# Reordering the second scan, down weights split once, and low parts of act on GpSimd, in a Mamba-2 layer kernel

## The reference, cut to what matters

```python
h = rmsnorm(x, ln1_w)
zxbcdt = h @ w_in.T                    # z, xs, B, C, dt
xBC = silu(causal_conv4(xBC) + conv_b)
dt = softplus(dt + dt_bias); a = -exp(A_log) * dt
# scan over 4 chunks of 128 rows, 4 heads, state carried from chunk to chunk:
#   Yd = ((C B^T) * decay) @ (x dt);  state = g * state + B^T (decay_end x dt);  Yo = (C state) * exp(cs)
h = x + (((Yd + Yo + D x) * silu(z)) @ w_out.T)
h2 = rmsnorm(h, ln2_w)
h = h + (silu(h2 @ gate_w.T) * (h2 @ up_w.T)) @ down_w.T        # inner width 1792 = 14 tiles
x = layernorm(x + h)
# second FFN with ternary weights, q(w) = round(clip(w / (mean|w| + eps), -1, 1)) * mean|w|, inner width 1376 = 11 tiles
x = layernorm(x + ((x @ q(w_gate).T) * (x @ q(w_up).T)) @ q(w_down).T)
```

## Time and profile before

| | us |
|---|---|
| median of 3 runs | 534.54 (533.47 to 535.83) |
| the profiled execution's own time | 534.14 |
| its span, first to last instruction | 532.3 |
| TensorE busy | 482.1 |
| DVE, POOL, ACT busy | 334.3, 252.0, 237.0 |
| mean granted TensorE clock | 0.978 |

### The profile page before, as it was taken

One profiled execution on the slowest core, in us unless ns is written; L12 is line 12 of the kernel. 1 busy time (PEld: TensorE's weight loads), 2 busy tenths in 40 slices (PEclk: granted clock), 3 DMA queues, 4 the chain that ended last, 5 costly groups with the idle time before them and its releaser, 6 DMA issues.

```text
span 532.3 us, 6133 instructions
## 1 busy us (share of the span) xinstructions
PE 482.1 (91%) x2060; PEld 378.7 (71%) x2060; DVE 334.3 (63%) x502; ACT 237.0 (45%) x438; POOL 252.0 (47%) x256
## 2 busy tenths in 40 slices
PE   6989999989779589899999989999898998999995
PEld 4767677756547467688877767887686786888884
DVE  4695777545564456658898879989944754332133
ACT  5577777565454536663333143435822331022300
POOL 5554575463732525766877554546403233123221
PEclk9999999989998969999999999999999999999998
DMA  7522021021211223443233214441410200110002
GB/s 249 186 82 79 6 75 60 20 78 61 81 64 54 79 100 135 151 171 118 81 118 120 79 66 172 158 166 72 138 61 1 78 21 0 41 39 1 1 1 79
DMA packets 15439, 44.47 MB, mean 84 GB/s; under 512 B 2480, under 2 KB 2480, under 8 KB 15408
## 3 DMA queue, kind: packets, MB, share of 16 engines
q1 hardware_dynamic: 15408, 44.08, 23.7%
HBM read 41.97 MB, written 2.10 MB: 83 GB/s over the span
## 4 chain that ended last, share of the span: by engine, by line
PE 66%; DVE 16%; issue 7%; ACT 4%; POOL 4%; DMA 2%; SPq 0%; POOLq 0%; DVEq 0%; ACTq 0%
PE psA L1553 8%; PE psA L1554 8%; PE psA L1347 5%; PE psA L1349 4%; PE psB L1562 4%; PE psB L1563 4%; DVE act_hl L1233 3%; PE psA L1335 3%; PE psA L1340 3%; PE psA L1336 3%; PE psA L1353 2%; PE psA L1355 2%; DVE q L1269 2%; PE psB L1528 1%; PE psB L1335 1%
## 5 line engine op out<-in xcount | busy, mean ns | idle before, releaser
L1553 PE MATMUL psA<-xT_h,q_gu 128*128 128x512 f32 x176 | 70.2, 399 | 1.5 <-DVE x L1281 1.5
L1554 PE MATMUL psA<-xT_l,q_gu 128*128 128x512 f32 x176 | 69.1, 392 | 0.0
L681 POOL TENSOR_TENSOR beta<-wsum,beta 128x512 fp32r<-128x512 f32 x28 | 38.9, 1411 | 37.3 <-ACT beta L844 37.3
L774 POOL TENSOR_TENSOR int_l<-prod_t,int_h 128x512 fp32r<-128x512 f32 x22 | 28.9, 1313 | 52.0 <-ACT int_h L987 51.9
L715 POOL TENSOR_TENSOR wst<-raw,wst 128x1024 fp32r<-128x1024 f32 x14 | 35.7, 2550 | 35.8 <-ACT wst L797 35.8
L982 ACT ACTIVATE gate_t<-psA 128x512 f32<-128x512 f32 x22 | 13.2, 598 | 83.0 <-PE psA L1554 83.0
L1299 DVE TENSOR_TENSOR prod_t<-gate_t,psA 128x512 f32<-128x512 f32 x22 | 15.1, 688 | 47.3 <-PE psA L1554 43.0
L1553 PEld LDWEIGHTS psA<-xT_h,q_gu 128*128 128x128 f32 x176 | 33.1, 188 | 10.2 <-issue 2.0
L1554 PEld LDWEIGHTS psA<-xT_l,q_gu 128*128 128x128 f32 x176 | 33.1, 188 | 7.3
L1233 DVE TENSOR_TENSOR act_hl<-act,act_hl 128x512 fp32r<-128x512 f32 x28 | 35.1, 1282 | 4.3 <-ACT act_hl L967 4.2
L1562 PE MATMUL psB<-q_dn,int_h 128*128 128x512 f32 x88 | 34.3, 390 | 2.1 <-issue 2.1
(11 more groups left out here) (234 smaller groups left out, 1386.0 us busy)
## 6 DMA issues: line engine op xcount, KB each, us to landing
raw<-in_f_gu_t SPq DMA_DIRECT2D x22, 512.0 KB, 3.2
raw<-in_w_gu_t SPq DMA_DIRECT2D x14, 512.0 KB, 3.3
raw<-in_w_dn_t SPq DMA_DIRECT2D x14, 512.0 KB, 3.2
raw<-in_f_dn_t SPq DMA_DIRECT2D x10, 512.0 KB, 3.6
raw<-in_w_gu_t SPq DMA_DIRECT2D x14, 256.0 KB, 2.7
raw<-in_w_in_t SPq DMA_DIRECT2D x5, 512.0 KB, 4.4
x<-in_hidden SPq DMA_DIRECT2D x8, 256.0 KB, 5.1
out<-x SPq DMA_DIRECT2D x8, 256.0 KB, 2.0
```

The source lines that it names most:

```text
L681: nc.gpsimd.tensor_tensor(beta[:, f % 2, 1, cols], wsum[:, f % 2, cols], beta[:, f % 2, 0, cols].bitcast(F32), ALU.subtract).then_inc(gb_l ...
L774: nc.gpsimd.tensor_tensor(int_l[:, f, :], prod_t[:, n % 2, :], int_h[:, f, :].bitcast(F32), ALU.subtract).then_inc(int_ready, 1)
L1553: nc.tensor.matmul(ps, w, seq(xT_h, k, b), start=k == 0, stop=False)
L1554: done = nc.tensor.matmul(ps, w, seq(xT_l, k, b), start=False, stop=k == KD - 1)
```

## The change

- The steps of the second scan: `tsplit` becomes `thigh` (ACT) and `tlow` (DVE) with places of their own. `thigh c` directly follows `turn2 1 c`, and `tlow c` comes after `outproj` and p2. `turn2` for batch 1 no longer uses the ACT copy `b_s`: DVE and ACT read PSUM. `t_ready` and `t_low` count twice per chunk, so that p6 waits for the first half only.
- `ga` loads come after the step instead of ahead of it, and ahead of the `sumgu` load of that step; `gb 0` follows `ga 10`, and `gsplit 0` comes last in step 9.
- In `outproj` POOL adds to `x` first and computes the reciprocal deviation afterwards.
- `dtturn 0` moves from inproj 0 0 to behind the convolution of inproj 0 3, `until 0 0` one step later. 30 dummy transposes instead of 14, and 11, 8 and 9 more behind `turn1` 1, 2 and 3.
- In stage 5 there is one `sum` load per f instead of up to two; `scales` at f = 7 instead of 4; the ternaries begin at f = 8 instead of 5, half a load (512 columns) per f.
- The down weights are loaded and split once (7 loads instead of 14) and stay in `dn_early` (nine tiles) and `dn_late` (five tiles) for both batches. In their place at 110592 was `q_dn`, so the ternaries of `w_down` go to `q8` in fp8 and are converted by ACT in `ffn 0 f` (`qcvdn`, six times).
- The low part of `act` is computed by POOL instead of DVE. `act 0 0` and `act 0 1` move ahead of p7 13.
- `ln1` is divided: `ln1a` (the addition that frees the PSUM bank) and `ln1` (the statistics).

```diff
-        if j == 0:
-            steps.append(("dtturn", 0))
+        if j == 3:
+            steps.append(("dtturn", 0))
...
     for s in range(NX + NZ):
         before, after, last = later.pop(0)
-        steps.append(load("ga", s + 1))
...
+            steps += before + first
+            for step in after:
+                steps.append(step)
+                if step[0] == "turn2":
+                    steps.append(("thigh", step[2]))
+            steps += second + [("tlow", c) for c in turned] + last
+        if s + 2 < NPRE:
+            steps.append(load("ga", s + 2))
         if s in (0, 2, 4, 6):
             steps.append(load(*sums.pop(0)))
...
+        if f == FM - 1:
+            steps += [("act", 0, 0), ("act", 0, 1)]
...
-        if f == 4:
+        if f == 7:
             steps.append(("scales",))
-        if f in (5, 7, 9, 11):
-            steps.append(load(*tern.pop(0)))
-    steps += [("act", 0, 0), ("act", 0, 1), ("p4", FM - 1), load("dn", 0, 1), ("m1", FM - 1)]
+        if f in (8, 10, 12):
+            loads_now, halves = ternary()
+            steps += loads_now
+        if f >= 8:
+            steps.append(halves.pop(0))
+    steps += [("p4", FM - 1), load("dn", 1), ("m1", FM - 1)]
 
     for f in range(FM):
-        if f % 2 == 0:
-            p = f // 2 + 2
-            steps.append(load("dn", 0, p) if p < FM // 2 else load("dn", 1, p - FM // 2))
+        if f % 2 == 0 and f // 2 + 2 < FM // 2:
+            steps.append(load("dn", f // 2 + 2))
         steps.append(("act", 0, f + 2) if f + 2 < FM else ("act", 1, f + 2 - FM))
         steps.append(("down", 0, f))
-        if f in (1, 4, 7, 9, 12):
-            steps.append(load(*tern.pop(0)))
+        if f % 2 == 0:
+            loads_now, halves = ternary()
+            steps += loads_now
+        steps.append(halves.pop(0))
...
-WARM_UP = 14
+WARM_UP = 30
+KEEP_WARM = {1: 11, 2: 8, 3: 9}
...
+        def dn_place_free(p):
+            if p == 0:
+                return done_p("p2", FM - 1)
+            if p == 1:
+                return done_p("p5", FM - 1)
+            return freed_a(("p74", FM - 1))
...
+                elif kind == "act":
+
+                    b, f = at
+                    n = FM * b + f
+                    pool.wait_ge(acth_ready, n + 1)
+                    high, low = act_hl[:, n % ACT_SLOTS, 0, :], act_hl[:, n % ACT_SLOTS, 1, :]
+                    nc.gpsimd.tensor_tensor(low, act[:, f, b, :], high.bitcast(F32), ALU.subtract)\
+                        .then_inc(actl_ready, 1)
...
                 elif kind == "outproj":
                     t = tile_of(step)
                     i = NT + t
+                    pool.wait_ge(*freed_b(step))
+                    nc.gpsimd.tensor_tensor(x[:, t, :], x[:, t, :], nrm[:, t % 2, :], ALU.add).then_inc(u_ready, 1)
                     pool.wait_ge(sq_ready, i + 1)
                     reciprocal_deviation(step, sq[:, i:i + 1], 1.0 / D)
...
+                elif kind == "thigh":
 
                     c = at[0]
-                    s.wait_ge(t_ready, c + 1)
-                    nc.scalar.activation(xT_h[:, :, chunk(NC + c)], b_s[:], ACT.Copy)
-                    nc.scalar.activation(tT_h[:, :, :, chunk(c)], t_f[:], ACT.Copy).then_inc(t_high, 1)
-                elif kind in ("turn1", "turn2", "ln1t"):
+                    s.wait_ge(t_ready, 2 * c + 1)
+                    nc.scalar.activation(tT_h[:, 0:2, :, chunk(c)], t_f[:, 0:2], ACT.Copy).then_inc(t_high, 1)
+                    s.wait_ge(t_ready, 2 * c + 2)
+                    nc.scalar.activation(xT_h[:, 0:2, chunk(NC + c)], t_f[:, 3], ACT.Copy)
+                    nc.scalar.activation(xT_h[:, 2:4, chunk(NC + c)], turned_b1(c)[:, 2:4, :], ACT.Copy)
+                    nc.scalar.activation(tT_h[:, 2, :, chunk(c)], t_f[:, 2], ACT.Copy).then_inc(t_high, 1)
...
+                elif kind == "quant":
+
+                    (what, f), half = at
...
+                    link(nc.vector.tensor_scalar(qtmp[:, cols], raw[:, n % RAW_SLOTS, cols], scl[:, 9 + w:10 + w], None,
+                                                 ALU.is_lt))
+                    last = nc.vector.scalar_tensor_tensor(
+                        out=q8[:, f, cols], in0=raw[:, n % RAW_SLOTS, cols], scalar=scl[:, 6 + w:7 + w],
+                        in1=qtmp[:, cols], op0=ALU.is_gt, op1=ALU.subtract, saturate=False)
```

More of the change, by code:

```diff
@@ L124, in build_schedule, with ternary @@
         before, after, last = later.pop(0)
-        steps.append(load("ga", s + 1))
         first, second = [("p1", s)], [("p2", s - 1)] if s >= 1 else []
-        if s == SCAN_ACT:
+        turned = [c for kind, *_, c in after if kind == "turn2"]
+        if s == NX + NZ - 1:
+            steps += before + after + first + [("thigh", NC - 1), ("tlow", NC - 1)] + second + [("gsplit", 0)]
+        elif s == SCAN_ACT:
             steps += before + second + after + first + last
-        elif s == NX + NZ - 1:
-            steps += before + after + first + [("tsplit", NC - 1)] + second
-        else:
-            steps += before + first + after + second + last
+        else:
+            steps += before + first
[6 more added lines that the diff above has]
+            steps.append(load("ga", s + 2))
         if s in (0, 2, 4, 6):
             steps.append(load(*sums.pop(0)))
-        if ("outproj", 1, NC - 1) in after:
-            steps += [load("gb", 0), ("gsplit", 0)]
-        for step in after:
-            if step[0] == "turn2" and step[2] < NC - 1:
-                steps.append(("tsplit", step[2]))
-    steps += [load("gb", 1), ("p1", NPRE - 1), ("p2", NPRE - 2), ("p2", NPRE - 1)]
+        if s == NX + NZ - 2:
+            steps.append(load("gb", 0))
+    steps += [("p1", NPRE - 1), ("p2", NPRE - 2), load("gb", 1), ("p2", NPRE - 1)]
     assert not later and NPRE == NX + NZ + 1
     tern = [("qgu", f) for f in range(FF)] + [("qdn", p) for p in range(FF // 2 + 1)]
+    def ternary():
+        which = tern.pop(0)
+        halves = 1 if which == ("qdn", FF // 2) and FF % 2 else 2
+        return [load(*which)], [("quant", which, i) for i in range(halves)]
     filler = {1: NPRE, 3: NPRE + 1, 5: NPRE + 2}
+    halves = []
     for f in range(FM):
@@ L162, in build_schedule @@
             steps.append(("silu0", f))
-        if sums:
-            steps.append(load(*sums.pop(0)))
         steps.append(("p3", f))
@@ L207, in build_schedule @@
             steps.append(("ffn", b, f))
+            if b == 0 and f in (1, 2, 3, 5, 7, 9):
+                steps.append(("qcvdn", dn_wide.pop(0)))
             if f >= 1:
                 steps.append(("inter", b, f - 1))
-            if tern and f in (3, 4, 6, 7, 9, 10):
-                steps.append(load(*tern.pop(0)))
+            if tern and f in (2, 4):
+                loads_now, halves = ternary()
+                steps += loads_now
+            if b == 0 and halves:
+                steps.append(halves.pop(0))
         steps.append(("inter", b, FF - 1))
@@ L217, in build_schedule @@
         steps.append(("ln2", b, NC - 1))
-    assert not (sums or tern or between or parts)
+    assert not (sums or tern or between or parts or dn_wide or halves)
     return steps, loads
@@ L223 @@
 RAW_SLOTS = 3
-WST_SLOTS = 3
+DN_EARLY = 9
 GA_SLOTS = 3
@@ L705, in _ @@
                 kind, at = step[0], step[1:]
-                if kind == "load" and at[0] in SPLITS:
+                if kind == "load" and LOADS[at[0]][0] == "out":
                     n = at[0]
@@ L789, in _ @@
                 kind, at = step[0], step[1:]
-                if kind == "load" and at[0] in INPROJ + SPLITS:
+                if kind == "load" and LOADS[at[0]][0] in ("in", "out"):
                     n = at[0]
@@ L1251, in _ @@
                     link(nc.vector.tensor_tensor(scl[:, 13:14], scl[:, 12:13], scl[:, 5:6], ALU.mult))
-                elif kind == "load" and LOADS[at[0]][0] in ("qgu", "qdn"):
-                    n = at[0]
-                    what, f = LOADS[n]
+                elif kind == "quant":
+                    (what, f), half = at
+                    n = LOADS.index((what, f))
+                    cols = slice(half * D, (half + 1) * D)
+                    w = half if what == "qgu" else 2
                     raw_arrived(v, n)
@@ L1281, in _ @@
                     nc.vector.tensor_tensor(x[:, t, :], bank_of(job), x[:, t, :], ALU.add).then_inc(freed(job)[0], 1)
-                    v.wait_ge(*freed(job))
+                elif kind == "ln1":
+                    t = at[0]
+                    v.wait_ge(*freed(("down", t // NC, t % NC)))
                     statistics(t, t)
```

197 lines of the change are left out of this document (100 added, 97 removed).

## The result

The changed kernel took **506.44 us** (median) against 534.29 us before (median of four): ratio 0.9472, 95% interval 0.9444 to 0.95. Three of its four executions took 505.89 to 506.52 us; the fourth took 1102.92 us at a granted clock of 1.00, is left out of the ratio, and no profile shows what held it up. The profiled execution took 506.52 us and its span 504.7. The forecast was 510.

A forecast was written before the change was run, and what follows sets the result against it. TensorE was taken as the bound, busy 482.1 of 532.3 us, leaving some 50 us to win. 2.6 + 0.5 + 15.7 + 7.6 - 6.4 + 4.0 = 24.0 won from 534.1 gave 510 us, range 501 to 521.

The forecast's parts named there:

- The 1.9 us for the warm-up: Start: the eight dt matmuls run at 2.4 instead of 1.2 GHz after a longer warm-up, saving some 1.9 us.
- The 0.7 for the dt chain: Start: moving the dt chain removes a 2.6 us wait at the fifth inproj, but all except some 0.7 comes back.
- DVE's total work before inproj 8 is the same: Start: the moved dt chain only delays conv 4, whose bank inproj 8 needs, so most of the 2.6 us returns.
- the large wait: Second scan: the last turn2's 8.7 us wait for norm2, blamed on queue order, shrinks by 7.5 us.
- The decay term (2.3): Second scan: with ga ahead of the sums, decay moves up by 1.0 and 1.3 us, winning 2.3.
- those of the halves: Products: three 1.2 us waits (3.7) behind four ternary operations on DVE go when half are done at a time.
- the 2.3 us for the weight load: Products: one sum load per f frees a full queue, so a 2.3 us weight-load wait goes, plus 1.6 of clock.
- the number (6.4): down 0: 6.4 us lost, from 8.3 of new stalls against 1.4 and 0.5 of waits gone.
- The third tile: down 0: the dn 2 load, split and act low part take 8.7 us, leaving TensorE 3.9 us short.
- The other 4.4: down 0: POOL needs 6.5 us per pair of tiles against TensorE's 5.44, 1.1 too much over four pairs.
- the ring: down 0 rival: loads, splits and ternaries run in series through three raw slots, 10.8 us per pair, total 539; chance 0.03.
- Where ffn waits for bank and last int_l nothing changes: ffn: those waits stay as they were, since ln1a 6 still stands behind ffn 0 0.

The follow-up runs named there:

- old_scan: Changed kernel with the second scan's old step order put back (thigh, tlow, gb 0, gsplit 0), new turn2 formulas kept: 513.0 us, ratio 0.9615.
- two_sums: Changed kernel with up to two sum loads per f in the products stage again and scales at f = 4: 508.74 us, ratio 0.9531.
- before_gsplit_late: Kernel before with one edit, gb 0 loaded behind step 8 and gsplit 0 last in step 9: 529.8 us, ratio 0.9938.
- act_low_on_vector: Changed kernel with the low parts of act on VectorE again in both passes, down weights still resident: 505.7 us, ratio 0.9473.
- ga_behind_sums: Changed kernel with the ternary sums ahead of the ga loads again in steps 0, 2, 4 and 6 of the second scan: 508.86 us, ratio 0.9535.

## Why the prediction was right, and where it was not

**Start: total right (3.1, measured 3.2), the two large terms wrong, which is luck.** The 1.9 us for the warm-up failed: leaving it out costs nothing that six timings show, and 0.6 us at p1 0. The forecast charged the clock of TensorE in a stretch where VectorE's convolutions set the pace a little later. The 0.7 for the dt chain was too small. The step "DVE's total work before inproj 8 is the same" failed: the chain's last operation had met GpSimd, and it no longer does. Undone by itself the chain costs 3.8 us (4.6 at p1 0 in the profile), of which some 3.4 are the clock that a wait of 3.67 us brings down; the kernel before had not paid this in its profile. The wait for the last turn2 of the first scan went from 1.18 to 0.78 us, 0.4 for the 0.5 forecast. So the chain's worth in the change is what is left of the 3.2 beside the 0.6 and the 0.4, some 2.2: an estimate, no run shows it.

**Second scan: right in sum (13.3 and 13.3), and in the chain of the large wait.** old_scan shows every link of it, and the last turn2 is 16.5 us earlier, as forecast. I had given the effect to three causes at once; the two moves turn out to be substitutes, and either alone has half or more of it. The decay term (2.3) measured 2.0. The clock behind the wait is real (0.65 and 0.84 in old_scan). The 0.8 of clock that was to come back at 160 us did not: the changed kernel has 0.85 at 130 us instead. Nor were the three windows of the earlier trace rows the only slow ones; the kernel before also shows 0.83 at 110 us, and so does the changed one.

**Products: 7.6 forecast; with the 2.4 us of clock behind the scan's wait and the 1.4 us at the entry of down 0 11.4 against 10.2.** The waits came back in the main: those of the sum loads with 2.3 and 1.2 us, those of the halves with two of three. Of the 2.3 us for the weight load only 1.4 were won, as 0.9 stay in the changed kernel. That the clock at 220 us hung on the first wait was a guess that two_sums and before_gsplit_late do not bear out.

**down 0: the number (6.4) by luck, half of the mechanism wrong.** The stage's 168 matmuls take 38.1 us at 0.227 each; before it had 1.2 us more, after 7.6, a difference of 6.4. The forecast had 1.9, of which 1.4 lie in the stage before, and 8.3; stage by stage it said 7.8 lost. The third tile: 2.90 us where 3.9 was forecast, by the chain as forecast. The other 4.4, GpSimd 1.1 us too slow in each of four pairs, failed: it is 0.3 to 0.6 too slow, at most waits of 0.97 (in which the ring has its part) and 0.26 us can come of it, and act_low_on_vector took the low parts away and gained 0.7. (It was over 9 tenths busy only from 310 us on, 8.2 and 8.1 of 10 us before.) In its place stand a clock of 1.2 GHz behind the stall (1.7 us), that wait of 0.97, and small ones. I had the ring as a rival at 0.03 and in series; a part of it is what happens. I also read the earlier trace rows wrongly for the compare:

```profile
L1317 DVE TENSOR_SCALAR qtmp<-raw,scl 128x512 bf16<-128x512 f32 x33 | 33.2, 1005 | 3.1 <-DMA raw<-in_f_gu_t 3.1
L765 POOL TENSOR_TENSOR act_hl<-act,act_hl 128x512 fp32r<-128x512 f32 x28 | 42.2, 1527 | 9.1 <-ACT act_hl L1017 9.1
```

Its mean was 482 ns and is 1005: it does wait for GpSimd, as the Trainium skill (SBUF — State Buffer, Who interferes with whom) says that tensor_scalar can. In the kernel before it had rarely met GpSimd, so its mean there said nothing of such meetings. What also failed is that each such meeting costs GpSimd the whole operation of VectorE. Two low parts took 2.55 us alone (1.28 each, where 1.31 was forecast) and 3.15 to 3.18 beside it, so 0.3 us for each, not 0.77; it is VectorE that loses, up to the length of GpSimd's operation.

**down 1: 3.5 of the 4.0 lie in this stage, measured 4.2.** The low parts' move gave nothing of it; which of the other edits did is open.

**ffn: 3.0 won where 0.5 was forecast,** and this is most of what the total of 510 was too high by. The wait of 2.1 us put down to "issue" was for the last ternary of the down weights, on VectorE, which ends at 445.16 in the kernel before:

```profile
444.41 0.75 DVE L1269 SCALAR_TENSOR_TENSOR q_dn<-raw,scl,qtmp 128x512 fp32r<-128x512 f32 x1
...
445.26 0.47 PE L1562 MATMUL psB<-q_dn,int_h 128*128 128x512 f32 x1 [2.07 <-issue]
```

In the changed kernel this wait is gone; its ternaries are made earlier, in halves, and converted by ACT. I had read the earlier trace rows for the waits for bank and int_l and passed it over: the step that failed is "Where ffn waits for bank and last int_l nothing changes", which left out this third wait. With the 0.55 for `x` 0.4 us of this stage stay open; no run here asks for them.

## What to carry to other kernels

When two edits could each remove a wait, undo them one at a time: the sum of a stage hides that they are substitutes, or that two errors cancel. A load in a ring of slots is released by its slowest user, so put nothing urgent behind the instruction that waits for its landing; moving the acts ahead of it was worth 3.0 us by the medians, 1.8 in its own stage, for one swapped line. And before giving an engine's clock or work a price, ask who sets the pace at the end of that stage.

## What the runs showed of the hardware

- A two-input VectorE operation, or this compare, that meets a GpSimd split takes about as long as what is left of that split, however small it is itself: 128x16 took 2.26 us instead of 0.17, the compare of 512 columns 2.5 to 2.6 instead of 0.48. GpSimd loses about 0.3 us per operation it shares with VectorE.
- The granted clock behind a wait is not the same in each execution of the same order of work: the wait of 2.5 us at p1 0 was followed by 0.83 at 110 us in the changed kernel and by 1.00 in ga_behind_sums, and the stall in down 0 by 0.87 (2.9 us) and by 1.00 (2.6 us). Waits of 3.67 and 7.82 us had windows of 0.66 and 0.65. The kernel before, too, kept its clock behind 2.64 us at the fifth inproj, and lost it with the same start behind 2.96 in before_gsplit_late. A window of 10 us at 0.83 costs 1.7 us. Over the 49 timed executions of the kernel before that stood beside the runs, time and mean clock have a correlation of -0.70, so the clock goes with about half of the scatter.
